# Recurrent two-layer block on one core: preparation and first layer put in one four-stage block, norms from one statistic, and what the second layer now computes itself

## What is computed

```python
x = L0_attn_inputs
xn = _layernorm(x, axis=-1)
s = _L0_attn_ref(xn, ...)     # a*state + (1-a)*b over the tokens, a, b, c = sigmoid/tanh of xn @ W
g = _silu(_L0_ffn_ref(xn, ...))   # gelu MLP 128 -> 512 -> 128 with binarised weights
x = x + s * g
xn = _layernorm(x, axis=-1)
s = _L1_attn_ref(xn, ...)
g = _silu(_L1_ffn_ref(xn, ...))   # experts: aff = xn @ centroids.T, eid = argmax, alpha = sigmoid(...)
x = x + s * g
# inside _L1_attn_ref:
ss = _rmsnorm(seq, store_norm_g)
lr = sigmoid(einsum('bnd,dh->bhn', ss, w_step)) * MAX_LR
cmean = ss.reshape(b, nc, c, d).mean(axis=2)          # chunks of 64 tokens
mom_gate = sigmoid(einsum('bnd,dh->bhn', cmean, w_mom))
decay = sigmoid(einsum('bnd,dh->bhn', cmean, w_decay))
sr = pad(_rmsnorm(seq, retrieve_norm_g)[:, c - 1:])    # moved by 63 tokens
gate = sigmoid(einsum('bnd,dh->bhn', sr, w_gate))
# inside _L1_ffn_ref: xln = layernorm(x) * ln_g[eid] + ln_b[eid]; out = x + alpha * ffn
```

## Time and profile before

| | us |
|---|---|
| median of three runs | 1193.63 |
| the profiled execution | 1189.44 |
| span of the profile (first to last instruction) | 1187.6 |
| busy: PE, DVE, ACT, POOL | 1100.7, 720.1, 679.8, 561.9 |
| TensorE's granted clock, mean over the span (1 is full speed) | 0.965 |
| end of the preparation, end of the first layer | 30.4, 169.1 |

### The profile page before, as it was taken

One profiled execution on the slowest core, in us unless ns is written; L12 is line 12 of the kernel. 1 busy time (PEld: TensorE's weight loads), 2 busy tenths in 40 slices (PEclk: granted clock), 3 DMA queues, 4 the chain that ended last, 5 costly groups with the idle time before them and its releaser, 6 DMA issues. The chain is left out here.

```text
span 1187.6 us, 20255 instructions
## 1 busy us (share of the span) xinstructions
PE 1100.7 (93%) x6649; PEld 917.9 (77%) x6650; DVE 720.1 (61%) x1892; ACT 679.8 (57%) x1369; POOL 561.9 (47%) x571
## 2 busy tenths in 40 slices
PE   4589869999999999999999899998999899999995
PEld 3356547788888888888888788887888788888884
DVE  4488856877655655655555455554555555556785
ACT  4666635566565565655555455554556455556663
POOL 3167753487764434444433343343434343344553
PEclk9888959999999999999999899999999999999998
DMA  9133330000300000000000000000000000002222
GB/s 209 38 89 90 89 115 1 1 21 21 98 24 1 2 16 10 10 10 18 9 10 7 20 8 10 8 9 19 8 8 9 19 8 10 3 5 77 88 88 72
DMA packets 57537, 40.32 MB, mean 34 GB/s; under 512 B 4595, under 2 KB 52061, under 8 KB 57310
## 3 DMA queue, kind: packets, MB, share of 16 engines
q1 hardware_dynamic: 53894, 32.10, 9.9%
q0 software_dynamic: 2304, 4.74, 1.2%
q10 hardware_dynamic: 1248, 2.23, 0.6%
HBM read 21.71 MB, written 15.50 MB: 31 GB/s over the span
## 5 line engine op out<-in xcount | busy, mean ns | idle before, releaser
L1105 DVE TENSOR_TENSOR p_sb<-bank,cf 128x512 f32<-128x512 f32 (+3 forms) x512 | 218.9, 483 | 1.1 <-PE bank L828 1.0
L1286 POOL TENSOR_TENSOR sq_rest<-sq,sq_high 128x450 f32<-128x450 f32 x64 | 67.2, 1050 | 247.1 <-ACT sq_high L995 247.1
L851 PE MATMUL bank<-p_sb,du_t 128*128 128x450 f32 (+3 forms) x512 | 131.1, 399 | 0.0
L851 PE MATMUL bank<-p_sb,err_t 128*128 128x450 f32 (+3 forms) x512 | 130.1, 397 | 0.0
L851 PEld LDWEIGHTS bank<-p_sb,err_t 128*128 128x128 f32 x512 | 85.0, 190 | 40.0 <-DVE p_sb L1105 16.9
L851 PEld LDWEIGHTS bank<-p_sb,du_t 128*128 128x128 f32 x512 | 82.0, 190 | 43.8 <-issue 29.8
L1138 DVE SCALAR_TENSOR_TENSOR acc<-bank,rg,acc 128x128 f32<-128x128 f32 x224 | 62.9, 344 | 84.6 <-POOL rg L1274 84.6
L1290 POOL TENSOR_TENSOR sq_low<-sq_rest,sq_mid 128x450 bf16<-128x450 f32 x64 | 66.6, 1041 | 100.1 <-ACT sq_mid L1012 99.9
L973 ACT ACTIVATE s_sb<-bank 128x512 f32<-128x512 f32 x64 | 38.3, 599 | 108.0 <-PE bank L828 108.0
L967 ACT ACTIVATE xs<-bank 128x450 f32<-128x450 f32 x64 | 35.1, 548 | 109.7 <-PE bank L851 108.5
L1174 DVE SCALAR_TENSOR_TENSOR du<-q_sb,bank 128x512 f32<-128x512 f32 x64 | 44.0, 688 | 87.5 <-PE bank L828 87.5
(11 more groups left out here) (304 smaller groups left out, 3193.0 us busy)
## 6 DMA issues: line engine op xcount, KB each, us to landing
x<-in_L_attn_inputs SPq DMA_DIRECT2D x16, 256.0 KB, 3.1
rows<-sorted_rows SPq DMA_DIRECT2D x40, 64.5 KB, 1.8
sorted_rows<-xl_all SPq DMA_DIRECT2D x1, 2064.0 KB, 14.7
x_rows<-x SPq DMA_DIRECT2D x8, 256.0 KB, 2.4
xn_rows<-xn SPq DMA_DIRECT2D x8, 256.0 KB, 2.4
xl_all<-xl SPq DMA_DIRECT2D x8, 256.0 KB, 3.4
ew<-in_L_ffn_w SPq DMA_DIRECT2D x8, 256.0 KB, 4.2
attn_out<-acc SPq DMA_DIRECT2D x7, 256.0 KB, 2.0
```

Source lines behind the costliest of these rows:

```text
L851: last = pe.matmul(out[:, P * i:QW], rows[:, i, :], p_sb[:, P_COL[i]:P_COL[i] + QW - P * i], start=False, stop=True, skip_group_check=True)
L1105: last = nc.vector.tensor_tensor(dst, src, w, ALU.mult)
L1286: nc.gpsimd.tensor_tensor(sq_rest[:], sq[:], sq_3[0][:], ALU.subtract).then_inc(g_rest, 1)
```

## The change

The functions prepare and layer0, the class At and the helpers less and pipelined are gone. In their place stands one function, first_layer, with one block and no barrier inside.

- The pipeline has four stages and 11 steps, written out: b1 statistics and normalisation of x, b2 the products and recurrence, b3 the MLP's second half, x1 and its statistics, b4 the norm and the gates' inputs.
- x of all 8 batches is loaded once into its own tile and stays; x1 is written over it. The weights' preparation is spread: the first layer's own weights in step 0, the transposes turn(0) to turn(3) in step 1, the gates' weights in step 1, the six groups of combined weights in steps 9 and 10, w_out one head a step on POOL.
- All three powers of a token come from the one variance of x1 (ve1 has three rows, taken in one POOL instruction of 12 elements). y is formed straight from x1 into xl_all, two of a batch's four tiles by ACT, two by POOL. xn1 is no longer made, and neither are its statistics. POOL normalises x (xn) in place of ACT.
- y is kept once: PE transposes xl_all, ACT writes the high part and DVE the low part of y_all. The gates' inputs are one product with 40 columns in high and low parts (12 products a batch). Chunk sums come from two matrices of ones (halves) over the products of all batches, at the end. gate_th is moved by 63 tokens for all batches in attend's step 0 (moved).
- In attend, DVE scales y in xl_all to xl (scale_rows, steps 3 to 10), so the scatters move to steps 4 to 11; count, blocks, places and shifted move to steps 1 to 4; last_sum forms xn1 again from x1 by four more instructions a batch; SP no longer writes or reads xn1_rows and no longer writes xl; the experts' second bias comes by one DMA.

```diff
-            def _(dve):
-                    if b4 is not None:
-                        for k in range(T):
-                            last = nc.vector.tensor_scalar(xn1[q][:, k, :], x1[q][:, k, :], mv1[:, k, 0:1], r1[:, k:k + 1], ALU.subtract, ALU.mult)
-                        stats(link, xn1[q], mv2)
-                        link(nc.vector.tensor_tensor(ve2[:, 0, :], mv2[:, :, 0], mv2[:, :, 0], ALU.mult))
...
-                    if b5 is not None:
-                        link(nc.vector.tensor_reduce(cm[:], y[:, 0:S].rearrange("p (c n) -> p c n", n=C), AX.X, ALU.add))
...
+                def step(t, b1, b2, b3, b4):
+                    if b4 is not None:
+                        nc.vector.scalar_tensor_tensor(nm[:], m.mv[:, rows, 0], -1.0, m.rr[:, 1, rows], ALU.mult, ALU.mult).then_inc(v_nm, 1)
+                    if b1 is not None:
+                        stats(x[b1], mv0)
+                    if t == 0:
+                        weights_of_first_layer()
+                    if t == 1:
+                        scaled()
+                    if b3 is not None:
+                        dve.wait_ge(c_thg, b3 + 1)
+                        link(nc.vector.scalar_tensor_tensor(z, thg, 1.0, z, ALU.add, ALU.mult))
...
+                        nc.vector.tensor_tensor(pr, st[:], z, ALU.mult).then_inc(v_pr, 1)
+                    if b4 is not None:
+                        dve.wait_ge(c_yh, b4 + 1)
+                        nc.vector.tensor_tensor(y_of(1, b4), m.bank[7][:], y_of(0, b4), ALU.subtract).then_inc(v_yl, 1)
...
+                        nc.vector.tensor_scalar(ve1[:, 0, :], mv[:, :, 1], LN_EPS, None, ALU.add)
+                        nc.vector.tensor_scalar(ve1[:, 1, :], mv[:, :, 1], 1.0 + RMS_EPS, LN_EPS * RMS_EPS, ALU.mult, ALU.add)
+                        nc.vector.tensor_scalar(ve1[:, 2, :], mv[:, :, 1], 1.0 + LN_EPS, LN_EPS * LN_EPS, ALU.mult, ALU.add).then_inc(v_var1, 1)
...
+                    if t == B + 1:
+                        nc.vector.scalar_tensor_tensor(m.w_v[1][:].rearrange("p h d -> p (h d)"), m.wkv[:, H * D:], m.neg_gs[:],
+                                                       m.w_v[0][:].rearrange("p h d -> p (h d)"), ALU.mult, ALU.subtract)
+                        for g in range(5):
+                            low(g)
+                    if t == B + 2:
+                        low(5)
...
+            def _(pool):
+                    if b4 is not None:
+                        for k in range(2, T):
+                            last = nc.gpsimd.tensor_scalar(m.xl_all[:, n, 0:D], x[b4][:, k, :], m.mv[:, n, 0:1], m.rr[:, 1, n:n + 1], ALU.subtract, ALU.mult)
+                    if b1 is not None:
+                        nc.gpsimd.tensor_tensor(r0[:], ve0[:], m.neg_half[:, 0:T], ALU.pow).then_inc(g_r0, 1)
+                        for k in range(T):
+                            last = nc.gpsimd.tensor_scalar(xn[:, k, :], x[b1][:, k, :], mv0[:, k, 0:1], r0[:, k:k + 1], ALU.subtract, ALU.mult)
...
+                    if b3 is not None:
+                        nc.gpsimd.tensor_tensor(m.rr[:, :, b3 * T:b3 * T + T], ve1[:], m.neg_half[:].rearrange("p (a t) -> p a t", t=T), ALU.pow).then_inc(g_r1, 1)
+                        nc.gpsimd.tensor_scalar(m.w_out[:, b3, :], m.wcomb[:, b3, :], m.gam1[:, b3:b3 + 1], None, ALU.mult)
...
+            def _(pe):
+                    if b4 is not None:
+                        pe.wait_ge(v_yl, b4 + 1)
+                        for k in range(T):
+                            for j, (u, v) in enumerate(((0, 0), (0, 1), (1, 0))):
+                                last = pe.matmul(m.bank[7][:, SMALL * k:SMALL * k + SMALL], m.y_all[u][:, b4, k * P:k * P + P], w_sm2[v][:],
+                                                 start=(j == 0), stop=(j == 2))
```

In attend:

```diff
                     if first_head(s) == 0:
+                        pe.matmul(moved, m.ahead, m.gate_th, start=True, stop=False)
+                        pe.matmul(moved[:, 0:NT - 1, :], m.behind, m.gate_th[:, 1:, :], start=False, stop=True).then_inc(p_gate, 1)
+                        pe.wait_ge(v_moved, 1)
+                    if first_head(s) == 1:
                         pe.matmul(QA[:, 0:NT * E], m.upper[:], flat, start=True, stop=True)
                         pe.matmul(QA[:, NT * E:2 * NT * E], m.ones[:], flat, start=True, stop=True).then_inc(p_cnt, 1)
...
+                def scale_rows(c):
+                    for t in range(c * T, c * T + T):
+                        last = nc.vector.tensor_scalar(m.xl_all[:, t, 0:D], m.xl_all[:, t, 0:D], m.rr[:, 2, t:t + 1], None, ALU.mult)
+                    last.then_inc(v_scaled, 1)
...
+                    if s is not None and isinstance(s[0], int) and 3 <= k < 3 + B:
+                        scale_rows(k - 3)
...
                 def last_sum(c):
+                    for t in range(T):
+                        last = nc.vector.tensor_scalar(fin_xn[q][:, t, :], fin_x[q][:, t, :], of(1, t), of(2, t), ALU.subtract, ALU.mult)
+                    link(last)
                     for t in range(T):
...
-                    t = T * (n_of(s) - 3) + part
+                    t = T * (n_of(s) - 4) + part
...
-                pe.wait_ge(v_made, 3)
                 heads(pe, step)
```

More of the change, by code:

```diff
@@ L51 @@
 SUMS = QW + 30
+SMALL = 5 * E
+ALPHAS = FB + 4
 class Chain:
@@ L145, in prepare, with steps @@
+        in_range = lambda b: b if 0 <= b < B else None
+        def steps(step):
+            for t in range(B + 3):
+                step(t, in_range(t), in_range(t - 1), in_range(t - 2), in_range(t - 3))
         with nc.Block() as block:
@@ L504, in _ @@
+                first_constants()
+                steps(step)
             @block.tensor
@@ L514, in step, with chunk_sums @@
+                def chunk_sums(first, last):
+                    for half in range(2):
+                        done = pe.matmul(m.bank[MD_BANK[half]][:, 2 * H * first:2 * H * last].rearrange("p (n h) -> p n h", h=2 * H),
+                                         halves[:, half, :], m.amd[:, first:last, E:], start=True, stop=True)
+                    done.then_inc(p_md, 1)
+                def step(t, b1, b2, b3, b4):
                     if b3 is not None:
-                        pe.wait_ge(c_thg, b3.i)
@@ new lines, in turned, with high, chunk_gates @@
+                def turned(g):
+                    act.wait_ge(p_kq, g + 1)
+                    nc.scalar.copy((m.kt, m.qt)[g // 2][:, four(g), :], quarter(KT_BANK[g])).then_inc(c_kq, 1)
+                def high(g):
+                    act.wait_ge(p_w, g + 1)
+                    nc.scalar.copy(weights(g)[0][:, four(g), :], quarter(W_BANK[g])).then_inc(c_high, 1)
+                def chunk_gates(first, last, n):
+                    act.wait_ge(p_md, n + 1)
+                    for half in range(2):
+                        done = nc.scalar.activation(m.md_th.rearrange("p (n a) h -> p n a h", a=2)[:, first:last, half, :],
+                                                    m.bank[MD_BANK[half]][:, 2 * H * first:2 * H * last].rearrange("p (n h) -> p n h", h=2 * H),
+                                                    ACT.Tanh, scale=0.5 / C)
+                    done.then_inc(c_md, 1)
@@ L616, in step @@
[L616 to L623 removed]
+                    if t == 1:
+                        turned(0)
+                        turned(1)
```

902 lines of the change are left out of this document (396 added, 506 removed).

## The result

The changed kernel takes 1159.66 us as the median of 4 runs (1159.43 to 1160.43), the kernel before 1192.83 (1191.91 to 1195.02, 4 runs); the ratio of their runs is 0.972, with a 95% interval of 0.9704 to 0.9737. The forecast was 1162.1, range 1149 to 1178. The profiled execution of after took 1159.49 us, with a span of 1157.70.

A forecast was written before the change was run, and what follows sets the result against it. TensorE was taken to bound attend, and chains the preparation and first layer. Terms of -43.3 ahead of attend, +4.4 early steps and +7.4 last batch made -31.5 us; from 1193.6 this gave 1162.1 us, range 1149 to 1178.

The forecast's parts named there:

- The start: First layer's start: xnf low at 13.0, 24.5 us gained; then 17.6 to first x1, some 6 more if weights land late.
- The pace: First layer's x1 starts 11.3 us apart, set by PE and DVE nearly together; seven intervals gain 14.0 us.
- The end of the first layer: From the last x1 to attend's first instruction: 16 us against 20.8, 4.8 gained.
- Attend's start: PE no longer waits for w1n low before its first product: costed at nothing, a gain up to 0.5 us possible.
- Steps 0 to 10: Early attend steps: moved count, shift of three values and scale_rows cost 4.4 us together; bounds 2 and 9.
- The moved piece: Attend's count moves to step 1 and stands again in step 0 for the gates: 1.5 us; three-value shift adds 0.2.
- scale_rows: Attend, DVE's four operations: 1.2 us in step 3, 0.4 each in steps 4 to 7, hidden in steps 8 to 10.
- The last batch: Attend's last batch: last_sum's four more operations cost 1.05 us in each of seven steps, 7.4 us; bounds 0 and 14.4.
- The first: Rival: attend hides all that DVE gets and the first layer's pace is DVE's 10.7; 1148 us, chance 0.13.
- The second: Rival: first layer's pace stays at 13.3, set by the PE, ACT and DVE round with a falling clock; 1176 us, chance 0.17.
- The fourth: Rival: POOL becomes the bound of the first layer, slower than before; 1202 us at 17 us a step, chance 0.02.
- The third: Rival: DVE and POOL exclude each other; last_sum costs 7 us more, scale_rows 5 more; 1174 us, chance 0.15.

The follow-up runs named there:

- run 7: Changed kernel with the gates' 12 narrow products made twice in each step of the first layer; 1174.26 us.
- run 8: Changed kernel with DVE's four statistics of xn made twice in each step of the first layer; 1160.11 us.
- run 9: Changed kernel with POOL's scaling of w_out made twice in each step of the first layer; 1161.85 us.
- run 1: Changed kernel with TensorE's wait for w1n low put back ahead of attend's first product; 1155.66 us.
- run 4: Changed kernel with scale_rows left out, so the routed rows lack that factor; 1156.71 us.
- run 2: Changed kernel with PE repeating the three w_v products three times before attend's product that waits for s_low; 1157.03 us.
- run 12: Changed kernel with TensorE's wait back, scale_rows and last_sum's subtractions (batches 1 to 6) ahead of du, and the first layer's end reordered; 1150.07 us.

## Why the prediction was right, step by step

- **The start.** xnf low at 13.0 forecast, 12.51 measured; 25.0 gained, not 24.5. From there to the first x1 17.2, not 17.6. The bounds for late weights were not needed. That the preparation was set by chains alone was misread: its loads kept the DMA engines busy for 0.96 of it. The sum did not use this reading, since it was made from the row of x itself.
- **The pace.** 11.3 forecast, 11.0 measured; 16.2 us gained over seven intervals, not 14.0. PE's order was forecast at 11.1 from the step of 11.97, which had 11.67 of work and 0.3 of idle time; less the 0.9 that leaves this is 10.8 of work. Measured are 10.28 of work and 0.72 of wait, so that the order comes out near 11.1 is in part luck: two errors of 0.4 to 0.5 cancel. The narrow products came at the 0.11 that was chosen between two bounds (run 7: 1.3 for 12). (The seven rows that left the place between ve and z hold 16 instructions, not 15; one of them, nm, only moved.) I called PE and DVE nearly equal; runs 7 to 9 show PE as the bound, POOL 0.4 and DVE 0.6 behind it. POOL's power took 2.66, not 2.9.
- **The end of the first layer.** 16 forecast, 17.5 measured. The step that failed is PE's share behind the last batch's y. The gates' products, put at 1.3, took 2.6, 0.21 apart, and the last combined product with its copy, put at 1.6, took 2.7 (119.51 to 122.19). The clock there is at its 1.2 GHz level, to which it fell behind PE's idle 2.5 us. The price of a loop was carried to a place where PE idles. The other terms of the 16 came out 0.8 less together.
- **Attend's start,** costed at nothing with a gain up to 0.5: it cost 1.9. This is the one term with the wrong sign. I had asked what the first product waits for, and not what PE does between it and the next wait; run 1 shows the wait that was taken away was free, and its removal was not. Its price is 1.9 in this trace; over the programs with the early start the first interval is 1.7 to 2.8 longer than the 12.4 before.
- **Steps 0 to 10.** 4.4 forecast, 4.4 measured (6.3 over nine intervals less the 1.9 of the first). The moved piece: 0.5 less in step 0 and 2.1 more in step 1 make 1.6, forecast 1.5 and 0.2. Step 4 is the longest of the early ones, as forecast, but by 2.7 and not 4. scale_rows: forecast 2.7, measured 2.5 in run 4, though not where I had it: the two later steps show 0.5 each, and the rest lies in step 4.
- **The last batch.** 7.4 forecast, 8.0 measured, but by other parts: 0.95 in six steps, not 1.05 in seven, since in the first DVE still waits 0.30 for PE ahead of ms and has no product of POOL beside it; and 2.3 in the last step, where I had nothing. There PE works at a lower clock (last section), after a wait of 2.0 us for xs low.
- **Rivals.** The first (attend hides all): steps 13.7 in the last batch did not come. The second (pace 13.3): x1 is 11.0 apart. The fourth: POOL's room is small but there. The third, an exclusive lock, was right in its mechanism and wrong in its price.

The 32 subtractions (minimum, median and maximum in ns) take 0.34 us in the median and 1.31 at most:

```profile
L1152 DVE TENSOR_SCALAR ew<-ew,token_q x32: 335/342/1309, 1044.0 to 1142.3; 128x128 f32<-128x128 f32 x32
```

These are the last two of the four in a step of the last batch, and POOL's two operations at that time:

```profile
1058.20 1.08 DVE L1152 TENSOR_SCALAR ew<-ew,token_q 128x128 f32<-128x128 f32 x1
...
1059.19 1.30 DVE L1152 TENSOR_SCALAR ew<-ew,token_q 128x128 f32<-128x128 f32 x1
```

```profile
1058.15 1.04 POOL L1236 TENSOR_TENSOR sq_low<-sq_rest,sq_mid 128x450 bf16<-128x450 f32 x1 [1.06 <-ACT sq_mid L932]
1059.14 1.28 POOL L1252 TENSOR_TENSOR ew<-ew 128x512 f32<-128x512 f32 x1
```

Each of the two starts 0.05 us behind an operation of POOL and ends 0.07 to 0.09 us behind that operation's end. The Trainium skill (SBUF — State Buffer, section "SBUF: two separate sides") calls the port pair of the two exclusive, held by one of them for its whole instruction, and these rows agree. But DVE then loses POOL's time less the work that it gets done, and not a time for each of its own operations: 0.73 beside 1.04 of POOL in the first step of the last batch (1.84 in place of 1.11), 1.70 beside 2.26 in the steps behind it, with eight operations in the way, and 1.8 before, with four. So the last batch lost no more to the lock than before, and the 12 us that the rival asked did not come.

Together: 44.9 gained ahead of attend, where 43.3 was forecast, and 14.9 given back, where it was 11.8; the spans differ by 29.9, the sum said 31.5. The forecast of 1162.1 was carried over from the median of 1193.6; the measured median is 2.4 lower. Part of this closeness is luck. Three terms err against the change (the first layer's end by 1.5, attend's start by 1.9, the last step by 2.3), the start and the pace err by 3.1 for it, and so do the six steps of the last batch, by 1.7. And the forecast added the 4.2 us by which before's profiled execution lay under its median, while the changed kernel's lies only 0.2 under its own: this puts the measured median below the forecast, though the profiled gain is 1.6 smaller than the sum.

## What to carry to other kernels

Before a wait is taken off an engine, look at where the engine will stand still instead: PE began attend 2.7 us earlier, had s_low no earlier, and lost 1.7 us to the lower clock. Work added to DVE at the end of a step, ahead of what PE waits for, cost 0.9 of its 1.1 us, though PE bounds the loop; in the gap ahead of an operation that waits for PE it cost next to nothing (steps of 13.7). Moving eight operations there, with their loads, gave 8 of the 12 us. Beside an engine that shuts another out, count the first one's time (here POOL's 2.3 us), not the second one's operations. And a price read in a busy loop (0.11 us a product) is not the price behind an idle stretch (0.21).

## What the runs showed of the hardware

- **The clock fell without an idle PE.** In run 7 PE was busy for 3.00 of 3.00 us at full clock (54 to 57) and had 0.54 over the next 3.40 while it was busy for 3.29 of them. The timeline shows no wait of PE in that step. All four falls of this run come 0.1 to 0.9 us behind the end of the 24 narrow products; in the two steps of the fifth and sixth interval the same 24 products were followed by the full clock. In the changed kernel, with 12 of them and 0.72 us of idle time in each step, it did not fall. Why is open.
- **The same wait, two clocks.** In the last step PE waits 2.0 us for xs low both in the changed kernel and in run 1. In the first it then works at half its clock for 6.5 us (until 1142.5), in the second at full clock. PE's timeline in the changed kernel:

```profile
1136.12 0.74 PE L739 MATMUL bank<-xs_high,s_high 128*128 128x450 f32 x1 [2.03 <-DVE xs_low L1060]
...
1140.41 3.08 PE L762 MATMUL bank<-p_sb,err_t 128*128 128x450 f32 x8
```

And in run 1:

```profile
1133.08 0.47 PE L739 MATMUL bank<-xs_high,s_high 128*128 128x450 f32 x1 [2.02 <-DVE xs_low L1059]
...
1136.10 2.01 PE L762 MATMUL bank<-p_sb,err_t 128*128 128x450 f32 x8
```

The same eight products take 3.08 and 2.01. The first layer's last interval is of the same kind: PE waits 1.17 us for a gelu in runs 2, 4, 8, 9 and 12 as in the changed kernel, and the eight products behind it take 3.67 in run 8 (x1 10.8 apart) and 5.37 in run 2 (12.5 apart), where the clock is 0.56 over the first 2 us. All four runs of the changed kernel lie within 1 us, and of its variants several spread over 2 to 6 us. What decides which clock follows a wait was not found.
- **POOL's operation keeps its length, DVE's does not.** POOL's product takes 1.27 to 1.32 with DVE's operations beside it, and 1.27 without them in the last step; DVE's four take 2.8 to 2.9 with POOL beside them and 1.1 without. POOL's power of 12 elements, though, took 3.26 beside DVE's splits and 2.66 in the steps of the loop.
